# Part of the loads on ScalarE's queue, the last queries' second half on ScalarE and GpSimd, and a shorter end

## What is computed

```python
q = (x @ wq).reshape(B, S, 16, 16); k = (x @ wk).reshape(B, S, 4, 16); v = (x @ wv).reshape(B, S, 4, 16)
q = q * cos + rotate_half(q) * sin;  k = k * cos + rotate_half(k) * sin
attn = softmax(einsum('bqkgd,bskd->bkgqs', qg, k) / 4)
x = layernorm(x + einsum('bkgqs,bskd->bqkgd', attn, v).reshape(B, S, E) @ wo)
h = silu(einsum('bsh,ih->bsi', x, Wg)) * einsum('bsh,ih->bsi', x, Wu)      # W = (int - 128) * scale
x = layernorm(x + einsum('bsi,hi->bsh', h, Wd))
```

## Time and profile before

| | us |
|---|---|
| median of three executions (lowest, highest) | 897.87 (894.81, 898.11) |
| the profiled execution | 896.11 |
| its span, first to last instruction | 894.3 |
| TensorE busy | 876.0 |
| VectorE, ScalarE, GpSimd busy | 743.9, 711.1, 268.9 |

### The profile page before, as it was taken

The page is one execution under the profiler, slowest core; times in us unless marked ns, Lnnn a source line. Parts: engine busy times, 40 slices in busy tenths (PEclk is TensorE's granted clock), DMA queues, the critical chain, the costliest instruction groups (busy, mean ns, idle before and its releaser), DMA issues.

```text
span 894.3 us, 16211 instructions
## 1 busy us (share of the span) xinstructions
PE 876.0 (98%) x5658; PEld 457.9 (51%) x5658; DVE 743.9 (83%) x1655; ACT 711.1 (80%) x929; POOL 268.9 (30%) x232
## 2 busy tenths in 40 slices
PE   9999999999999999999999999999999999999996
PEld 3334444444444444434444444444436888888885
DVE  5688999999999999999999999999955455665545
ACT  2466999999999999999999999999985466555564
POOL 6564430045334010001001000210104665665555
PEclk9997999999999999999999999999999999999998
DMA  8874543423342122122223212121112010110001
GB/s 301 251 208 103 148 116 89 98 73 86 103 115 58 46 77 71 52 70 67 53 60 82 74 43 78 45 69 31 35 55 57 25 49 24 48 48 25 25 24 48
DMA packets 53458, 69.98 MB, mean 78 GB/s; under 512 B 17344, under 2 KB 26560, under 8 KB 53376
## 3 DMA queue, kind: packets, MB, share of 16 engines
q1 hardware_dynamic: 50280, 65.53, 26.4%
q0 software_dynamic: 864, 3.15, 1.1%
q10 hardware_dynamic: 2232, 0.25, 0.2%
HBM read 46.74 MB, written 16.25 MB: 70 GB/s over the span
## 4 chain that ended last, share of the span: by engine, by line
PE 89%; DVE 5%; ACT 2%; SPq 2%; DMA 2%; issue 1%; POOL 0%; POOLq 0%; DVEq 0%
PE pv_bank L1395 27%; PE ring_bank L1305 24%; PE pair_bank L1454 13%; PE pair_bank L1524 12%; PE pv_bank L1550 3%; PE ring_bank L1550 3%; PE ring_bank L1405 2%; DVE block_max L869 2%; PE pair_bank L1343 1%; ACT probs L1203 1%; DMA ident<-identity 1%; PE ring_bank L1420 1%; DMA k_max<-k_parts 0%; PE pair_bank L1305 0%; DVE inv_sums L962 0%
## 5 line engine op out<-in xcount | busy, mean ns | idle before, releaser
L1203 ACT ACTIVATE probs<-pair_bank 128x1024 f32<-128x1024 f32 x512 | 495.9, 1024 | 45.6 <-PE pair_bank L1454 45.5
L869 DVE TENSOR_REDUCE block_max<-ring_bank 128x1 f32<-128x384 f32 x854 | 486.5, 609 | 14.4 <-PE ring_bank L1305 4.1
L1305 PE MATMUL ring_bank<-k_max,q_sb 48*128 48x512 f32 x1122 | 310.1, 443 | 3.8 <-DVE block_max L865 2.6
L1305 PEld LDWEIGHTS ring_bank<-k_max,q_sb 48*128 48x128 f32 x1122 | 149.1, 185 | 267.1 <-DVE block_max L869 119.7
L1395 PE MATMUL pv_bank<-probs,v_all 128*17 128x512 f32 x2048 | 271.4, 602 | 0.7 <-ACT probs L1203 0.7
L1454 PE MATMUL pair_bank<-q_sb,k_sb 50*128 50x512 f32 x1024 | 221.5, 427 | 0.8 <-ACT probs L1203 0.7
L1063 DVE SCALAR_TENSOR_TENSOR hid<-pair_bank,up_s,silu 128x512 f32<-128x512 f32 x63 | 47.1, 748 | 85.1 <-ACT silu L1265 85.1
L1454 PEld LDWEIGHTS pair_bank<-q_sb,k_sb 50*128 50x128 f32 x1024 | 98.5, 186 | 27.2 <-ACT probs L1203 6.4
L774 POOL TENSOR_TENSOR hid_l<-hid,hid_h 128x512 fp32r<-128x512 f32 x63 | 81.7, 1296 | 86.4 <-ACT hid_h L1244 85.7
L689 POOL TENSOR_TENSOR attn<-attn,inv_rows 128x1024 f32<-128x1024 f32 x7 | 16.7, 2388 | 300.8 <-DMA inv_rows<-inv_d 300.8
L865 DVE CUSTOM_DVE_ANT_0 above<-ring_bank,above 128x512 f32<-128x512 f32 x128 | 88.1, 689 | 5.0 <-ACT above L1151 4.9
(11 more groups left out here) (147 smaller groups left out, 862.9 us busy)
## 6 DMA issues: line engine op xcount, KB each, us to landing
k_max<-k_parts SPq DMA_DIRECT2D x96, 96.0 KB, 3.1
q_sb<-q_parts SPq DMA_DIRECT2D x64, 128.0 KB, 2.8
k_sb<-k_parts SPq DMA_DIRECT2D x96, 64.0 KB, 2.4
attn<-xT SPq DMA_DIRECT2D x8, 512.0 KB, 7.6
q_parts<-high SPq DMA_DIRECT2D x16, 256.0 KB, 3.6
q_parts<-low SPq DMA_DIRECT2D x16, 256.0 KB, 3.9
q_sb<-q_parts SPq DMA_DIRECT2D x64, 64.0 KB, 2.9
attn<-pv_sb SPq DMA_DIRECT2D x128, 32.0 KB
```

The source lines that it names most:

```text
L869: dve.reduce_max(block_max[half % 2][:, col:col + 1], bank[:, 0:width], axis=AX.X).then_inc(ring_used, 1)
L1203: act.activation(probs[t % 2][:, 2 * pr:2 * pr + 2, :], pair_bank[pr][:], ACT.Exp, scale=D ** -0.5).then_inc(probs_ready, 1)
L1305: pe.matmul(bank[:, 0:last - first], q_sb[k][rows, i, qt * P:(qt + 1) * P], k_max[k // QH][rows, kind * CH + first:kind * CH + last], star ...
```

## The change

1. **Start.** The first block of x comes in two DMAs with a semaphore each (`x_parts_loaded`); TensorE waits for each where it uses it. The weights `wkv` are issued on ScalarE's queue, ahead of everything there. TensorE makes two warm-up matmuls, not three.
2. **First keys and queries.** ScalarE's queue issues the first queries' four loads (`first_queries`), behind its `high_part(1, 1)`. On SP both halves of the gap are stored together, then the two rounded halves of block 1, then the first keys' loads, then the low halves.
3. **Prologue.** `copy_v_rows` and `copy_k_rows` of an odd block stand ahead of `high_part(m - 1, 0)` on ScalarE. On VectorE both `rotary_q` calls stand one group of maxima earlier. The ring's bank numbers are turned round (`early_banks`, `bank_index`).
4. **Border.** ScalarE copies the last half of the queries out of `pv_bank` (`copy_q_last`) into the place of x's block 5; GpSimd multiplies it (`products_last`) and rounds both halves of block 7 (`high_last`). VectorE and ScalarE no longer do this work within the loop. `products_k(1)` moves behind it and waits for the turn of half 1; `swap_strips(1)`, with SP's wait for the prologue's end, moves behind `load_shift(0, 1)`. In step 0 TensorE makes the second pair of scores after one block of maxima, not two.
5. **End.** The second half's tiles are both normalised by VectorE as (y - mean) * rstd, without an offset; ScalarE does tiles 0 and 1.

The diff, cut to its core:

```diff
@@ bank_index
-            return pos % EARLY_BANKS if pos < early_entries else (0, 1, EARLY_BANKS)[pos % BANKS]
+            return pos % EARLY_BANKS if pos < early_entries else (3, 0, EARLY_BANKS)[pos % BANKS]
@@ sync
-            sp.dma_start(wkv_sb[:], wkv.rearrange("(k p) n -> p k n", p=P)).then_inc(wkv_loaded, 16)
-            load_x(0)
+            for k in range(KE):
+                sp.dma_start(x_in[0][:, k, :], xT_v[:, k, 0:CH]).then_inc(x_parts_loaded[k], 16)
...
                     elif m == 1:
                         store_k(0)
-                        store_gap(0, (0,))
+                        store_gap(0)
                         store_q(m, 0, (0,))
-                        store_gap(0, (1,))
-                        first_queries()
+                        store_q(m, 1, (0,))
+                        first_keys()
                         store_q(m, 0, (1,))
-                        first_keys()
-                        store_q(m, 1)
+                        store_q(m, 1, (1,))
...
                             load_kv(0, 1)
-                            swap_strips(1)
-                        store_q(m, 0)
-                        store_q(m, 1)
+                            for part in range(2):
+                                store_q(m, 0, (part,))
+                                store_q(m, 1, (part,))
...
-            for slot in range(4):
-                sp.wait_ge(stored[slot], 16 * 2 * B)
-            sp.wait_ge(v_used, 2 * B)
+            def prologue_over():
+                ...
                         load_shift(p + 1, 0)
+                    if first and k == 0:
+                        prologue_over()
+                        swap_strips(1)
@@ gpsimd
+            def products_last():
+                cols = slice(CH, S)
+                pool.wait_ge(q_last_ready, 1)
+                pool.wait_ge(q_tables_loaded[1], 16 * 2)
+                pool.wait_ge(rot_ready, 2 * (BLOCKS - 1))
+                pool.tensor_tensor(by_sin[0][:], q_last, sinq_sb[:, cols], ALU.mult).then_inc(q_last_parts, 1)
+                pool.tensor_tensor(by_cos[1][:], q_last, cos_sb[:, cols], ALU.mult).then_inc(q_last_parts, 1)
...
+            def high_last(j):
+                slot = 2 + j
+                pool.wait_ge(rot_ready, 2 * (BLOCKS - 1) + j + 1)
+                pool.wait_ge(stored[slot], 16 * 2 * (B - 1))
+                pool.tensor_copy(high[slot][:], rotated[j][:]).then_inc(last_high_ready, 1)
...
-                if m == BLOCKS - 2:
-                    products_k(1)
+            after_turn(1)
+            products_k(1)
...
-                pool.tensor_tensor(offset2[:, part], minus_mean2[:, part], rstd2[:, part], ALU.mult).then_inc(tail_offset[h], 1)
+                if h == 0:
+                    pool.wait_ge(tail_rstd[0], 1)
+                    pool.wait_ge(tail_minus, 1)
+                    pool.tensor_tensor(offset2[:, part], minus_mean2[:, part], rstd2[:, part], ALU.mult).then_inc(tail_offset, 1)
@@ vector
+                rotary_q(m, 0)
                 early_maxima(m, 2)
-                rotary_q(m, 0)
                 early_maxima(m, 3)
-                early_maxima(m, 4)
                 if m < BLOCKS - 1:
                     rotary_q(m, 1)
+                early_maxima(m, 4)
...
-                    if n == 3 and g == 0:
-                        rotary_q(BLOCKS - 1, 1)
...
-            dve.wait_ge(tail_offset[1], 1)
-            dve.tensor_scalar(y[1][:, TT - 1, :], y[1][:, TT - 1, :], rstd2[:, TT - 1:TT], offset2[:, TT - 1:TT], ALU.mult, ALU.add).then_inc(tail_last, 1)
+            dve.wait_ge(tail_rstd[1], 1)
+            for t in (2, 3):
+                dve.tensor_scalar(y[1][:, t, :], y[1][:, t, :], mean_var2[:, t, 0:1], rstd2[:, t:t + 1], ALU.subtract, ALU.mult).then_inc(tail_last, 1)
@@ scalar
+            def copy_q_last():
+                act.wait_ge(proj_ready, 3 * BLOCKS)
+                act.activation(q_last, pv_bank[:], ACT.Copy).then_inc(q_last_ready, 1)
...
+            act.dma_start(wkv_sb[:], wkv.rearrange("(k p) n -> p k n", p=P)).then_inc(wkv_loaded, 16)
...
-                            if (g, pr) == (2, 1):
-                                high_part(BLOCKS - 1, 0)
-                            if (g, pr) == (3, 1):
-                                high_part(BLOCKS - 1, 1)
@@ tensor
-                    pe.wait_ge(parts_ready, Q_PARTS * BLOCKS)
+                    pe.wait_ge(q_last_ready, 1)
...
                             scores(0)
                             maxima(0)
-                            maxima(1)
                             scores(1)
-                            for i in range(2, len(entries)):
+                            for i in range(1, len(entries)):
                                 maxima(i)
```

More of the change, by code:

```diff
@@ L44 @@
 BLOCKS = 2 * B
-WARM = 3
+WARM = 2
 MIXED = (0, 2, 4, 6)
@@ L108, in layer @@
         by_sin = [sb(f"by_sin{c}", [P, CH], fp32, one) for c in range(2)]
+        rotated = [sb(f"rotated{c}", [P, CH], fp32, one) for c in range(2)]
+        q_last = attn[:, FIRST, 0:CH]
+        key_signs = sb("key_signs", [P, HKV * D], fp32, one)
+        high = [sb("high0", [P, CH], f32r, one)]
         v_rows = [sb(f"v_rows{c}", [P, CH], fp32, one) for c in range(2)]
-        rotated = [sb(f"rotated{c}", [P, CH], fp32, one) for c in range(2)]
-        key_signs = sb("key_signs", [P, HKV * D], fp32, one)
-        high = [sb(f"high{c}", [P, CH], f32r, one) for c in range(4)]
+        high += [sb(f"high{c}", [P, CH], f32r, one) for c in range(1, 4)]
         low = [sb(f"low{c}", [P, CH], f32r, one) for c in range(4)]
@@ L186, in layer @@
         weights_loaded, ident_loaded = sem("weights_loaded"), sem("ident_loaded")
-        x_loaded = [sem(f"x_loaded{m}") for m in range(BLOCKS)]
+        x_parts_loaded = [sem(f"x_parts_loaded{k}") for k in range(KE)]
+        x_loaded = [None] + [sem(f"x_loaded{m}") for m in range(1, BLOCKS)]
         proj_ready, v_used, v_rows_ready = sem("proj_ready"), sem("v_used"), sem("v_rows_ready")
@@ L220, in layer @@
         out_stored = [sem(f"out_stored{c}") for c in range(2)]
-        tail_sum, tail_stats, tail_mv, tail_eps = ([sem(f"{n}{h}") for h in range(2)] for n in ("tail_sum", "tail_stats", "tail_mv", "tail_eps"))
-        tail_rstd, tail_offset, tail_y = ([sem(f"{n}{h}") for h in range(2)] for n in ("tail_rstd", "tail_offset", "tail_y"))
-        tail_last = sem("tail_last")
+        tail_sum, tail_stats, tail_mv, tail_eps, tail_rstd = ([sem(f"{n}{h}") for h in range(2)] for n in ("tail_sum", "tail_stats", "tail_mv", "tail_eps", "tail_rstd"))
+        tail_minus, tail_offset, tail_y, tail_last = sem("tail_minus"), sem("tail_offset"), sem("tail_y"), sem("tail_last")
         last_gu, last_silu, last_hid, last_hid_h, last_hid_l = ([sem(f"{n}{h}") for h in range(2)] for n in ("last_gu", "last_silu", "last_hid", "last_hid_h", "last_hid_l"))
@@ L384, in load_shift @@
                         write_shift(k, o, b, sp)
-            def first_queries():
-                for slot in range(2):
-                    sp.wait_ge(stored[slot], 16 * 2)
-                load_q(0, 0, sp)
             def first_keys():
@@ L402, in store_q @@
                 cols = slice(c * CH, (c + 1) * CH)
-                for part, buf, ready, count in [((0, high, hi_ready, 2 * m + j + 1), (1, low, lo_ready[j], m + 1))[q] for q in parts]:
+                highs = (0, high, last_high_ready, j + 1) if m == BLOCKS - 1 else (0, high, hi_ready, 2 * m + j + 1)
+                for part, buf, ready, count in [(highs, (1, low, lo_ready[j], m + 1))[q] for q in parts]:
                     sp.wait_ge(ready, count)
@@ L500, in spread_inverses @@
                     sp.dma_start(inv_rows[h * D:(h + 1) * D, :], inv_d[h:h + 1].broadcast_to([D, S])).then_inc(inv_loaded, 16)
-            for slot in range(4):
-                sp.wait_ge(stored[slot], 16 * 2 * B)
-            sp.wait_ge(v_used, 2 * B)
+            def prologue_over():
+                for slot in range(4):
+                    sp.wait_ge(stored[slot], 16 * 2 * B)
+                sp.wait_ge(v_used, 2 * B)
             def attention(p, first, last):
@@ L1158, in early_takes, with first_queries @@
                         difference(key[0], key[1] // 4, (key[1] % 4,))
+            def first_queries():
+                for slot in range(2):
+                    act.wait_ge(stored[slot], 16 * 2)
+                load_q(0, 0, act)
+            act.dma_start(wkv_sb[:], wkv.rearrange("(k p) n -> p k n", p=P)).then_inc(wkv_loaded, 16)
             for m in range(BLOCKS):
@@ L1166, in _ @@
                     gap_high()
+                if c and b:
+                    copy_v_rows(b)
+                    copy_k_rows(b)
                 if m:
@@ L1276, in _ @@
             norm2_apply(2 * B - 2, 0)
-            for t in range(TT - 1):
-                act.wait_ge(tail_offset[t // 2], 1)
```

(11 more changed lines are left out.)

42 lines of the change are left out of this document (29 added, 13 removed).

## The result

The changed kernel took **898.83 us** in the median of 20 executions (895.84 to 901.70) beside 896.56 of the kernel before (20 executions, 894.57 to 899.18). The ratio is **1.0027** with a 95% interval of 1.0019 to 1.0036: slower by a quarter of a percent, where I had forecast a gain of 1.2 us. The profiled execution took 900.70 us, span 898.6.

The account below looks back on a forecast made before the run. It took TensorE, busy in 98% of the span, as the bound: gains of -7.9 us, less a queue wait of 3.0 and a clock fall of 3.7, sum to -1.2, a median of 896.7 us (range 889.5 to 901.5).

Parts of the forecast that it names:

- Clock at the border, -3.7: Steps 1 to 7 behind the border: with TensorE's two waits gone the clock stays at full speed, saving 3.7 us.
- First keys, -1.3: Prologue: the first keys' loads start 1.3 us earlier on SP, so TensorE's whole wait of 1.3 us goes.
- v's rows, -0.4: Prologue: ScalarE copies v's rows before its rounding, so TensorE's wait of 0.5 goes; 0.4 us saved.
- the border's waits, -2.2: Step 0: VectorE's two products leave and second scores come sooner; of 2.6 us of waits about 0.4 stays.
- Start, -0.1: Start of the kernel: first projections begin earlier by at most a warm-up matmul; 0.1 us saved (0 to 0.5).
- end, -0.2: End of the last half: VectorE starts 0.3 earlier without the offset and one small operation goes; 0.2 us saved.
- The queue: SP's order: swaps behind half 1's shift rows delay half 2's, so TensorE waits 3.0 us at its first score.
- Clock behind the queue's wait, +3.7: Behind half 2's first score: the idle wait makes the clock fall as at the border, costing 3.7 us.
- the wait, but the clock stays: Rival at half 2: wait of 3.0 without a fall, half 3 waits 1.4 more; -3.5, 894.4 us; chance 0.14.
- the rival of two falls: Clock falls at the border as before and again behind the queue's wait; 900.4 us, 901.7 at worst; chance 0.15.
- the first: Rival that SP's queue is no bound at half 2, so all is kept: -7.9, 890.0 us; chance 0.18.

Follow-up runs that it names:

- lag_alone: The kernel before with only the move: swap_strips(1) behind load_shift(0, 1), products_k(1) behind the turn of half 1; 901.07 us, ratio 1.0051.
- keys_shift_fill: `keys_first` with half 0's shift rows loaded ahead of half 2's queries, plus eight 48x512 filler matmuls at the border; 890.28 us, ratio 0.9955 to the kernel before.
- best_fill: `fill_fast_more` with the loads of the scales and wo moved behind half 3's shift loads; 889.55 us, ratio 0.9926 to the kernel before.
- changed_again: The changed kernel run once more, unaltered, beside the kernel before; 899.71 us, ratio 1.0030.
- q_on_sp: The changed kernel with the first queries' loads back on SP and block 1's order of before; 899.16 us, ratio 1.0031 to the kernel before.
- scales_late: The changed kernel with the loads of the scales and wo moved behind half 3's shift loads; 898.68 us, ratio 1.0022 to the kernel before.
- keys_first: `swaps_early` with the first keys' loads ahead of block 1's two stores of highs on SP; 891.60 us, ratio 0.9953 to the kernel before.
- swaps_early: The changed kernel with swap_strips(1) ahead of load_shift(0, 1) again and products_k(1) before the turn of half 1; 893.76 us, ratio 0.9966 to the kernel before.
- fill_fast: `keys_first` with half 0's shift rows ahead of half 2's queries, plus four 128-row fp32r fillers at the border; 892.35 us, ratio 0.9951 to the kernel before.
- fill_fast_more: `fill_fast` with eight fillers (four, two, two) in place of four; 891.96 us, ratio 0.9955 to the kernel before.
- both_undone: `swaps_early` with the first queries' loads on SP again and block 1's order of before; 892.59 us, ratio 0.9972 to the kernel before.

## Why the prediction was wrong

The time lay in the range, but the sign was not the forecast's: +2.3 us where I said -1.2. Step by step:

- **Clock at the border, -3.7: the step that failed.** I argued that with the two waits gone nothing was left that the prologue didn't also have. The waits went, and the clock fell all the same, at 66.9 and 67.1, and stayed low for 6.8 and 10.2 us in the two profiles of the changed kernel (before: at 69.4, for 10.2; in `lag_alone`, with the old border, at 67.0, so the earlier fall is not the change's). It even fell without waits (`keys_shift_fill`), and it stayed up in four of the five profiles with fillers of 128 rows. My comparison with the keys' wait took the length of waits as all that matters and left aside what TensorE does between them: from 63.9 to 70.6 us it makes only 48- and 50-row matmuls. What makes the clock fall there stays open.
- **The size of that term** was right for a fall of ten microseconds: from step 0's product with v to the turn of half 1 the kernel before took 13.18 us and `best_fill`, at full clock, 9.57. But the length was one profile's. By the stages, a spell of low clock of 6.8 us behind half 2's wait cost 24.55 - 18.86 - 2.59 = 3.1 us (`lag_alone`) and 23.73 - 18.87 - 2.06 = 2.8 (`changed_again`), one of 3.4 us 1.5 to 1.6 (`q_on_sp`, `scales_late`). The kernel before, in the 25 executions beside `changed_again`, had mean clocks from 0.987 to 0.993; the profile's 0.991 was not its best. So even a border without a fall would probably have won less than 3.7 in the median.
- **First keys, -1.3: failed.** The loads did start 1.7 earlier (24.01 against 25.75), but landed in 5.1 and 4.6 us (median of the six), not 3.4. The wait was 2.2 and 1.4. I gave such a slowing half a microsecond, for the queries' loads beside them; it took all, and its cause was another: the stores of both high halves now stood directly ahead of the loads, and without them the same loads land in 2.8 (`keys_first`). These two terms are what the gain lacks: -7.9 without 3.7 and 1.3 is -2.9, and `swaps_early`, the change without its queue, measured -2.6.
- **v's rows, -0.4, and the border's waits, -2.2: right.** 0.5 gone, and 2.6 became 0.8. In the stages only 1.5 of it shows; in this profile the clock fell earlier, which slows that stretch. The cast took 0.17 us, not 0.65, and GpSimd had ended its work at 73.2, six microseconds ahead of it; in the kernel before it was subtracting (81.60 to 82.88) when the cast ran.
- **Start, -0.1, and end, -0.2: nothing against them.** TensorE's first projection started 0.6 us sooner (5.15 against 5.75), but VectorE's first product stood between 8.7 and 10.2 us in the profiles of kernels with this start, at 9.70 and 10.22 in the two with the old one: the gain is less than one profile can tell. The last stage of the table is 0.1 shorter, which is also less than that.
- **The queue: right.** 24.4 us from turn to shift rows (24 forecast), a wait of 2.5, 2.1 and, alone, 2.6 us (3.0, with 2.0 to 4.3 around it). The place was off, 107 for 102, since the border hadn't won what it was to win. `swaps_early` gave back 5.95 us, against the 6.7 of my terms.
- **Clock behind the queue's wait, +3.7: right that it falls in most, too large.** It fell at half 2 in one profile and not in the other, where half 3's wait then came with its own fall. The forecast's own alternative, "the wait, but the clock stays", thus has another end: the wait only moves one half on, 2.2 us for the 1.4 that I gave it, and with the fall.

What came is the rival of two falls, with a chance of 0.15: the border keeps its fall and the queue's wait brings another. With 3.0 us of wait it had +2.5, and +2.3 came, but that close only by luck: the keys' 1.3 was not won, and the fall and the wait behind the queue cost less than it had. That the time lay in the forecast's range says as little, since it reached from this rival to the first. The rival's point of decision was wrong too. I had it hang on TensorE's waiting twice for over a microsecond in step 0; it waited once for 0.5 and once for 0.3.

## What to carry to other kernels

When a step is moved to free one engine, ask for the DMAs that it issues where in their queue's order they come to stand, and count that queue to the next point where somebody waits for it: here four swaps moved past the shift rows cost 4.7 us by themselves and hid a gain of 2.6. A gain ahead of a full queue is returned at its next deadline, so the order is to empty the queue first and quicken the engine second. And take no term for a clock that rises again from a single profile: change what is thought to make it fall, and look at several executions.

## What the runs showed of the hardware

- The clock fell at the border in all 14 profiles of kernels without fillers of 128 rows, at 64.8 to 69.4 us and for 3.4 to 13.8, and in one of the five with them (`fill_fast`). It fell with no wait over 0.3 us near it (66.2 to 69.6 in `keys_shift_fill`), when TensorE had made only 48- and 50-row matmuls since 61.4. Whether it is the rows, or the 3.8 us by which the fp32 fillers hold the border's work back, isn't settled: `fill_fast` fell and `fill_fast_more` did not.
- In the profile of the changed kernel a wait of 2.49 us (106.7 to 109.2) and the keys' of 2.16 (to 33.1) were followed by no fall. Six other waits at the first scores of a half, of 1.91, 2.06, 2.07, 2.17, 2.59 and 2.65 (`scales_late`, `changed_again`, `fill_fast`, the changed kernel, `lag_alone`, `q_on_sp`) were followed by one each, 0.1 to 1.7 us after their end. So the length of a wait does not tell by itself. The Trainium skill (TensorE: Matmul & The Clock Gate, Part 1) says that the point of change varies from run to run of one kernel; the two profiles of the changed kernel agree.
- The six loads of 96 KB took 2.8 to 3.0 us to land (median of the six) in the nine profiles with no store of the queries right ahead of them and another queue's loads beside them, 3.4 and 3.6 with the stores spread out ahead and all loads on one queue (`q_on_sp`, `both_undone`), and 4.5 to 5.1 in the six profiles behind two stores of 256 KB with another queue's loads beside them.
